# Feed-forward half of an attention block: transposes moved from TensorE to the DMA queue, and one step of the rounding folded into an addition

## The reference, cut to what matters

```python
def block_quant(v, m_bits, bk):
    vb = v.reshape(*lead, K // bk, bk)
    amax = jnp.max(jnp.abs(vb), axis=-1, keepdims=True)
    e = jnp.floor(jnp.log2(jnp.maximum(amax, tiny)))
    scale = jnp.exp2(e - m_bits)
    return (jnp.round(vb / scale) * scale).reshape(v.shape)

def lowprec_linear(x, w, b, m_bits, bk):
    return jnp.einsum('bsk,nk->bsn', block_quant(x, m_bits, bk), block_quant(w, m_bits, bk)) + b

x = x + attention(layernorm(x), ctx, ctx, ...)
h = gelu(lowprec_linear(layernorm(x), w_fc, b_fc, 3, 32))     # 256 -> 1024
x = x + lowprec_linear(h, w_proj, b_proj, 3, 32)              # 1024 -> 256
```

## Time and profile before

| | us |
|---|---|
| median of 3 runs | 261.62 (261.4 to 262.09) |
| profiled execution | 264.13 |
| its span, first to last instruction | 262.3 |
| busy in the span: PE / DVE / ACT / POOL | 229.7 / 195.0 / 174.0 / 119.6 |
| mean granted clock of TensorE, share of full speed | 0.964 |

### The profile page before, as it was taken

How to read it: one execution, slowest core, us unless ns; L and a number is a source line. 1 busy time by engine, 2 the same in 40 slices (tenths; PEclk the granted TensorE clock), 3 DMA queues, 4 the chain that set the end, 5 groups by cost and what they waited for, 6 DMA issues and landing times.

```text
span 262.3 us, 6399 instructions
## 1 busy us (share of the span) xinstructions
PE 229.7 (88%) x2302; PEld 173.7 (66%) x2310; DVE 195.0 (74%) x433; ACT 174.0 (66%) x462; POOL 119.6 (46%) x120
## 2 busy tenths in 40 slices
PE   7996998997999989999999999988769599579964
PEld 7794776775777768677777777776436357346743
DVE  4343358677577789869978977588898995999981
ACT  1351766768777777766776876798845636658971
POOL 2700004105905826732621750460816494569892
PEclk9996899999999999999999999999998959999998
DMA  6692821752352244225125215204003201011112
GB/s 196 153 284 59 262 54 39 230 104 60 78 98 70 56 88 93 66 63 104 40 51 91 60 40 96 62 18 74 2 2 53 53 20 41 8 36 42 40 47 75
DMA packets 37999, 20.40 MB, mean 78 GB/s; under 512 B 13124, under 2 KB 37712, under 8 KB 37968
## 3 DMA queue, kind: packets, MB, share of 16 engines
q1 hardware_dynamic: 34896, 17.17, 28.0%
q10 hardware_dynamic: 3072, 2.82, 3.6%
HBM read 7.61 MB, written 2.11 MB: 37 GB/s over the span
## 4 chain that ended last, share of the span: by engine, by line
PE 55%; DVE 15%; issue 10%; POOL 6%; DMA 6%; SPq 5%; ACT 2%; ACTq 1%; POOLq 0%; DVEq 0%
PE bank L1000 15%; PE bank L1069 8%; PE s_banks L1057 7%; PE s_banks L1051 5%; DVE probT L776 5%; POOL hq L673 4%; PE bank L1111 4%; PE bank L1092 4%; PE s_banks L1218 2%; DMA QS<-full 2%; DMA w_rows<-in_L_xattn_Wq 2%; SPq L250 2%; DVE hrn L942 2%; PE bank L976 2%; SPq L286 2%
## 5 line engine op out<-in xcount | busy, mean ns | idle before, releaser
L426 ACT ACTIVATE prob<-s_banks,negm 128x128 f32<-128x128 f32 x256 | 72.9, 368 | 36.5 <-DVE negm L768 34.8
L768 DVE TENSOR_REDUCE negm<-s_banks 128x4 f32<-128x512 f32 x64 | 43.8, 686 | 30.9 <-PE s_banks L1057 30.7
L776 DVE COPY probT<-bank 128x512 f32<-128x512 f32 x64 | 43.9, 686 | 7.3 <-PE bank L1069 7.3
L1069 PE MATMUL bank<-ident_f,prob 128*128 128x128 f32 x256 | 40.8, 282 | 8.1 <-DVE probT L776 8.1
L673 POOL TENSOR_TENSOR hq<-hrn,h_mag 128x1024 bf16<-128x1024 f32 (+1 forms) x17 | 31.2, 1836 | 20.8 <-DVE hrn L942 20.5
L1069 PEld LDWEIGHTS bank<-ident_f,prob 128*128 128x128 f32 x256 | 27.3, 140 | 16.5 <-issue 12.8
L1000 PE MATMUL bank<-cT,wT 128*128 128x256 f32 x128 | 32.2, 397 | 0.0
L562 POOL TENSOR_TENSOR rs<-ve,neg_half 128x2 f32<-128x2 f32 x8 | 5.6, 702 | 51.3 <-DVE ve L721 51.0
L571 POOL TENSOR_TENSOR XQ<-xr,x_mag 128x512 bf16<-128x512 f32 x8 | 8.4, 1048 | 41.8 <-DVE xr L840 41.8
L512 ACT ACTIVATE s_banks<-s_banks 128x512 f32<-128x512 f32 x32 | 17.9, 581 | 14.1 <-PE s_banks L1218 13.7
L1000 PEld LDWEIGHTS bank<-cT,wT 128*128 128x128 f32 x128 | 24.7, 203 | 3.0
(11 more groups left out here) (122 smaller groups left out, 422.2 us busy)
## 6 DMA issues: line engine op xcount, KB each, us to landing
oden<-oT SPq DMA_DIRECT2D x60, 64.0 KB, 2.4
KS<-full SPq DMA_DIRECT2D x32, 64.0 KB, 2.3
VS<-full SPq DMA_DIRECT2D x64, 32.0 KB, 1.9
out<-full SPq DMA_DIRECT2D x16, 128.0 KB, 1.7
QS<-full SPq DMA_DIRECT2D x29, 64.0 KB, 2.3
X<-in_x ACTq DMA_DIRECT2D x1, 1536.0 KB, 7.6
cbuf<-in_ctx SPq DMA_DIRECT2D x6, 256.0 KB, 4.5
fc_rows<-in_L_ffn_w_fc SPq DMA_DIRECT2D x1, 1024.0 KB, 5.9
```

The source lines that it names most:

```text
L426: ins = nc.scalar.activation(prob[:, k % 4, u, s, :], s_banks[:, 2 * (k % 2) + u, s * P:(s + 1) * P], ACT.Exp, bias=negm[:, k % 4, u, s:s ...
L768: V.tensor_reduce(negm[:, k % 4, :, :], s_banks[:, 2 * (k % 2):2 * (k % 2) + 2, 0:2 * P].rearrange("p u (s t) -> p u s t", s=2), axis=AX.X ...
L776: V.tensor_copy(probT[:, k % 4, :, :, :].rearrange("p u s t -> p (u s t)"), pt_bank(k)[:, :])\
L1069: ins = T.transpose(pt_bank(k)[:, (2 * u + s) * P:(2 * u + s + 1) * P], prob[:, k % 4, u, s, :], ident_f[:, :])
```

## The change

The hidden layer of tiles 4 to 13, all weights, and the rounded rows of all tiles are transposed by DMAs that SP issues (`dma_start_transpose`). Tiles 0 to 3, 14 and 15 keep the way over PE and ACT. The down projection and all that follows it (copy, residual, store) comes two tiles later as before up to tile 3, and three tiles later from tile 4 on; `hqT` has three buffers in place of two, and tile 13's result is finished after the loop. The multiplication by the magic factor leaves DVE's queue: the exponent instruction sets the highest mantissa bit as well, which makes it 1.5 times the power of two, and the addition multiplies by `RAISE` itself (`scalar_tensor_tensor`). POOL still needs the product; ACT computes it (`magic`). The last two tiles add their residual in place, into `X`, and no longer wait for a store.

```diff
+RAISE = 2.0 ** (23 - MBITS)
...
-        xqT = [sb(f"xqT{n}", [P, KC, P], bf16) for n in range(2)]
+        xqT = sb("xqT", [P, B, KC, P], bf16)
...
+        def half_up(eng, dst, src):
+
+            return eng.tensor_scalar(dst.bitcast(i32), src.bitcast(i32), 0x7F800000, 0x00400000, ALU.bitwise_and,
+                                     ALU.bitwise_or)
...
+        BY_DMA = 4
+
+        def result_of(t):
+
+            return t - 2 if t <= BY_DMA + 1 else t - 3
...
+            def transpose_rows(p):
+
+                sp.wait_ge(sm["xq_done"], p + 1)
+                sp.dma_start_transpose(xqT[:, 2 * p:2 * p + 2, :, :].rearrange("p b k t -> p (b k) t"),
+                                       XQ[:, 2 * p:2 * p + 2, :].rearrange("p b e -> p (b e)"))\
+                  .then_inc(sm[f"xqt{p}"], 16)
+
+            def transpose_fc():
+                sp.wait_ge(sm["fc_ready"], 4)
+                for n in range(2):
+                    sp.dma_start_transpose(wfcT[:, 4 * n:4 * n + 4, :, :].rearrange("p a k m -> p (a k) m"),
+                                           fc_q[:, 4 * n:4 * n + 4, :].rearrange("p a e -> p (a e)"))\
+                      .then_inc(sm["wt_in"], 16)
+
+            def transpose_pj(f):
+                sp.wait_ge(sm["fc_ready"], 6 + 2 * f)
+                sp.dma_start_transpose(wpjT[:, :, f * P:(f + 1) * P], pj_q[:, f, :]).then_inc(sm["wt_in"], 16)
...
+                if last:
+                    transpose_fc()
+                    for p in range(NPAIR - 3):
+                        transpose_rows(p)
+                    for f in range(2):
+                        transpose_pj(f)
...
+            def tile(t, par, first, last):
+                if BY_DMA <= t < B - 2:
+                    sp.wait_ge(sm["hq_done"], t + 1)
+                    sp.wait_ge(sm["f2_done"], t - 2)
+                    sp.dma_start_transpose(hqT[t % 3][:, :, :], hq[par][:, :]).then_inc(sm[f"hqt{t % 3}_in"], 16)
+                if t in (1, 5, 9):
+                    transpose_rows(NPAIR - 3 + t // 4)
+                if t >= 2 and t != BY_DMA + 2:
+                    store(result_of(t), result_of(t) % 2)
...
+                magic(t, par)
+                if t >= 2 and t != BY_DMA + 2:
+                    copy_rows(result_of(t), result_of(t) % 2)
+                if 1 <= t <= BY_DMA or last:
+                    copy_th(t - 1, 1 - par)
+
+            def magic(t, par):
+
+                act.wait_ge(sm["h_exp_done"], t + 1)
                 if t >= 2:
-                    copy_rows(t - 2, par)
-                if not first:
-                    copy_th(t - 1, 1 - par)
+                    act.wait_ge(sm["hq_done"], t - 1)
+                nc.scalar.activation(h_mag[par][:, :], h_exps(t), ACT.Copy, scale=RAISE).then_inc(sm["h_mag_done"], 1)
...
                     pool.wait_ge(sm["h_round"], 2 * t + 2 if not last else 2 * t + 1 + n)
+                    pool.wait_ge(sm["h_mag_done"], t + 1)
                     if t >= 2:
-                        pool.wait_ge(sm["th_done"], t - 1)
+                        if t - 2 < BY_DMA:
+                            pool.wait_ge(sm["th_done"], t - 1)
+                        else:
+                            pool.wait_ge(sm[f"hqt{(t - 2) % 3}_in"], 16 * ((t - 2 - BY_DMA) // 3 + 1))
...
-                    V.tensor_tensor(blocks(hrn[par][:, 512 * n:512 * n + 512]), blocks(bank[2 * par + n][:, :]),
-                                    spread(h_mag[par][:, 512 // BLK * n:512 // BLK * (n + 1)], 512 // BLK), ALU.add)\
+                    V.scalar_tensor_tensor(blocks(hrn[par][:, 512 * n:512 * n + 512]),
+                                           spread(exps[:, 512 // BLK * n:512 // BLK * (n + 1)], 512 // BLK), RAISE,
+                                           blocks(bank[2 * par + n][:, :]), ALU.mult, ALU.add)\
                         .then_inc(sm["h_round"], 1)
...
             def ffn_up(t, par):
-                pe.wait_ge(sm["tq_copied"], t + 1)
+                if t % 2 == 0:
+                    pe.wait_ge(sm[f"xqt{t // 2}"], 16)
+                if t == 0:
+                    pe.wait_ge(sm["wt_in"], 64)
...
             def tile(t, par, first, last):
                 if t > 0 and not last:
                     ffn_up(t + 1, 1 - par)
-                if t < B - 2:
-                    trans_q(t + 2)
-                if t >= 2:
-                    ffn_down(t - 2, par)
-                if not first:
+                if t >= 2 and t != BY_DMA + 2:
+                    ffn_down(result_of(t), result_of(t) % 2)
+                if 1 <= t <= BY_DMA or last:
                     trans_h(t - 1, 1 - par)
```

More of the change, by code:

```diff
@@ L73, in build_program @@
         pj_q = sb("pj_q", [P, KC, HID], bf16)
-        wfcT = sb("wfcT", [P, KC, HID], bf16)
+        wfcT = sb("wfcT", [P, HID // P, KC, P], bf16)
         wpjT = sb("wpjT", [P, HID // P, E], bf16)
@@ L126, in build_program @@
         h_amax = sb("h_amax", [P, HID // BLK])
-        h_exp = sb("h_exp", [P, HID // BLK])
+        h_exp = [sb(f"h_exp{n}", [P, HID // BLK]) for n in range(2)]
         h_mag = [sb(f"h_mag{n}", [P, HID // BLK]) for n in range(2)]
-        hqT = [sb(f"hqT{n}", [P, HID // P, P], bf16) for n in range(2)]
+        hqT = [sb(f"hqT{n}", [P, HID // P, P], bf16) for n in range(3)]
         res = [m[:, 0:E] for m in full[0:2]]
@@ L333, in _, with store @@
             move_last()
-            def tile(t, par, first, last):
+            def store(t, par):
                 if t < B - 2:
@@ L1146, in step @@
                     transpose_probs(k - 1)
-                if last:
-                    trans_weights(0)
-                    trans_weights(1)
-                else:
+                if not last:
                     project(i + 1, 0)
@@ L1158, in step @@
                 transpose_probs(k + 1)
-                if last:
-                    trans_weights(2)
-                else:
+                if not last:
                     project(i + 1, 1)
@@ L1249, in ffn_down @@
                 for a in range(HID // P):
-                    ins = T.matmul(o, hqT[par][:, a, :], wpjT[:, a, :], start=False, stop=(a == HID // P - 1))
+                    ins = T.matmul(o, hqT[t % 3][:, a, :], wpjT[:, a, :], start=False, stop=(a == HID // P - 1))
                 ins.then_inc(sm["f2_done"], 1)
@@ L1285, in _ @@
                 if a % 4 == 0:
-                    pe.wait_ge(sm["th_copied"], B + a // 4)
-                ins = T.matmul(down_b[:, 0:E], hqT[1][:, a, :], wpjT[:, a, :], start=False, stop=(a == HID // P - 1))
+                    pe.wait_ge(sm["th_copied"], BY_DMA + 2 + a // 4)
+                ins = T.matmul(down_b[:, 0:E], hqT[0][:, a, :], wpjT[:, a, :], start=False, stop=(a == HID // P - 1))
             ins.then_inc(sm["f2_done"], 1)
```

150 lines of the change are left out of this document (47 added, 103 removed).

## The result

The kernel after takes 270.09 us against 261.86 for the kernel before beside it, a ratio of 1.031 (95% interval 1.023 to 1.039). Measured once more on another chip it is 269.40 against 264.01, 1.020 (1.013 to 1.027). So it is slower, by 2 to 3%. The prediction, 258.2 with a range from 257.0 to 265.5, is wrong.

The account below looks back on a forecast made before the run. DVE was taken to set the late tiles' pace, with four engines nearly full. DVE -4.1, POOL +0.5, end +0.5, start -0.3 sum to -3.4 us, from 261.62 to 258.2; range 257.0 to 265.5.

Parts of the forecast that it names:

- the start: Last attention step to first up projection: transposes by DMA let it start at 188.45 instead of 188.75, -0.3 us.
- the wait for POOL: At the start: the fifth row pair waits for POOL until 184.2, the last two weights behind it, landing at 188.45.
- Rival A: SP's queue at the start: transposes hold the first up projection; 265.5 us with 2 us per 256 KB; chance 0.22.
- c: Time that 256 KB of transposing DMA take of SP's queue; slower from 1.65 us on, under 1 by a load's rate.
- DVE's 2.68: Late tiles: DVE's time per tile falls from 2.91 to 2.68 us without the multiplication.
- the fused addition: DVE's rounding: addition with the product inside costs what the plain addition costs, 0.65 us a half.
- C: DVE's rounding in 16 tiles: fused addition at half the rate, 1.29 us more a tile, about 278 us; chance 0.03.
- Tile 5's 0.68: DVE in tile 5: its slow multiplication goes, saving 0.68 us, part of the 4.1 us less on DVE.
- POOL's own term: Tiles 7 to 14: POOL's floor of 2.61 us and pair 7's rows give back 0.5 us.
- The hidden layer's landing: Tiles 6 to 15: 256 KB transposes land in 3.15 us, inside the room of 3.45, so 0 us.
- Rival B: TensorE falls to its lower clock in tiles 6 to 10, up to 1.9 us a tile; one tile: 260.0; chance 0.18.
- The end: After tile 14's subtraction: the wait for a store moves to tile 13's result copy, 6.6 instead of 6.1 us, +0.5.

Follow-up runs that it names:

- The merged one: The kernel after with the rows of pairs 0 to 3 transposed by one DMA of 512 KB in place of four of 128 KB: 266.34 us, 1.013.
- the best version with early weights (in place, filled): Kernel after, weights' transposes issued one and two attention steps earlier, result added and stored in place, ten small TensorE matmuls in tiles 2, 3, 6 to 13: 261.62 us, 0.990.
- the version in place: Kernel after with weights' transposes issued one and two attention steps earlier, and POOL adding the result into the row block, stored from there: 261.40 us, 0.992.

## Why the prediction was wrong

**The step that failed is the start.** It said: "issued by 182.8 if an issue takes the 0.6 us of the present ones". An issue of a transposing DMA takes 1.23 to 1.37 us of the queue. The eight DMAs began at 173.88 (forecast 174.1) and ended at 179.0 (179.2), as worked out; then nine times 1.34 instead of 0.6 gave 191.07, and with 1.9 us of landing 192.97. In place of -0.3 the term is +4.2 on the clock of the trace, and +5.8 after the anchor. The row pairs were ready at 183.86, so the wait for POOL that I let decide was none.

**Rival A happened, but by another price.** I had counted 6.5 shares of 256 KB, by the byte, and held c under 1 from a load's rate. The queue charges per DMA: nine, not 6.5. A's sum would need c = 1.84 for 192.98, while 256 KB took 1.23 to 1.37, which would not have reached A's own threshold of 1.65. All prices that I had were of plain DMAs, and none of them bounded this kind. The Trainium skill, "DMA: Bandwidth & Descriptors" (section "Latency and other measured facts"), has 261 GB/s for a transposing DMA with a non-contiguous middle dimension, measured on one kernel, and 350 to 400 for the contiguous case. The merged one lies at the first figure: 512 KB in 1.99 us are 264 GB/s. With 128 KB in 1.27 us it is 103, and a rate alone misleads for small transposes.

**What was missing behind it.** The longer wait left TensorE idle for 5.3 us, and the first up projections ran at the lower clock: 1.3 us more by tile 0 (7.06 against 5.76). Keeping TensorE busy gave 1.5 us of that stretch back (8.44 to 6.92), 0.8 of it still there at tile 0.

**The tiles.** DVE's 2.68 was right (2.69), the fused addition too, and C falls. Tile 5's 0.68 was not saved: its exponents alone took 1.64 us in the kernel after, more than twice the 0.65 of the multiplication that went. From tile 0 to 15 the best version with early weights (in place, filled) gains 59.09 - 56.33 = 2.8 us, not 3.6 (4.1 less POOL's 0.5). POOL's own term was right in kind: where the stores no longer hold up ACT and the hidden layer goes by DMA, the end hangs on POOL, 1.3 to 1.9 us behind DVE at tile 15. The hidden layer's landing was right in the median (3.1 for 3.15), and POOL waited for it once, 1.7 us; TensorE, which was to find its operand there, waited once in the kernel after (0.8 us) and three times in the version in place (2.5 us). What was wrong is the sentence on what queues behind it: "only the store three tiles older, which has two tiles to land". Stores behind transposes take 0.58 us of the queue and up to 1.51, and ACT, with its gelu, waited 4.6 us for them in the profiled execution. Rival B happened too: granted clock 0.50 from 230.7 to 240.6, and 3.91 us for tile 10 (240.87 to 244.78, ends of the rounding).

**The end.** +0.5 was forecast, and 0.5 was lost behind tile 15; ACT's copy of a result did wait for a store there (1.15 us).

**The base.** I took the profiled execution's 264.13 as unrelated to the change and went down from 261.62. In the later comparisons the kernel before stood at 263.1 to 264.4; the execution was the typical one. With the start mended, the result in place and the hidden layer on TensorE, the ratio 0.988 is -3.3 us, nearly the sum of -3.4 that I gave. That is luck: this version leaves out the hidden layer's DMA, which my sum was made for, and its terms differ from mine.

**Slips in the sums.** From 128 to 1024 KB the landing grows by 3.5 us over 896 KB, 4.0 us per 1024 KB and not 3.9. By my own price of 5 us per us the estimate of "some 30 us more" for the tiles would be 35, (10.5 - 3.45) x 5. Neither changes the forecast.

Left open: how much each of the clock's drops costs in the kernel after itself, since its stores and its clock come together there; why the late tiles lose 2.55 us in one of its executions and 0.32 in the other; and whether any of the versions at 0.988 to 0.992 is better than the others, which these intervals don't tell.

## What to carry to other kernels

Price a new kind of DMA by its place in the queue, per DMA, before its transfer, and count what stands ahead of the one that is waited for: nine short transposes behind one another were worth 6 us, and issuing four of them where the queue idled took the loss away. When a queue carries both latency-critical loads and stores, free the buffers by something other than the store's landing; here that was worth some 0.6%, barely clear of the noise. Work taken from one of four nearly full engines pays only as far as the next one, here 0.06 us a tile.

## What was unexpected in the hardware

- A transposing DMA between two places in SBUF holds SP's queue for 1.23 to 1.37 us at 128 and at 256 KB, and 1.99 us at 512 KB; 256 KB land after 3.0 to 3.4 us, at most 4.8 beside stores.
- A store issued behind them takes 0.58 us of the queue instead of 0.33, at worst 1.51, and lands after 2.0 us in the median instead of 1.7.
- An instruction on 32 columns of DVE that reads and writes SBUF (tile 5's exponents) took 1.64 us beside POOL's subtraction and ended with it, at 222.86 against 222.83. The same instruction took 0.18 us in tile 0, where POOL stood idle, and 0.19 with its operand in PSUM. No run tests the cause.
